# Order of small pieces of work around a fixed stream of matmuls: weight chunks, partial sums, table loads and loads of k

## The reference

```
ek = exp(min(k, 30));  ekv = ek * k;  euk = exp(min(u + k, 30))
nf, nb = forward and backward scans a = a * decay + ekv;  df, db = the same of ek
num = nf + nb - ekv + euk * k;  den = df + db - ek + euk
y = sigmoid(r) * num / max(den, 1e-8) * (0.8 + 0.2 * tf)
```

```
out = x + y @ W.T + bias + sum over experts of coeff[e] * (y @ A[e].T) @ B[e].T
```

## Time and profile before

| | us |
|---|---|
| median of 3 runs | 652.41 |
| profiled execution | 651.88 |
| its span | 650.0 |
| TensorE busy (matmul) | 586.4 |
| VectorE | 498.6 |
| ScalarE | 381.6 |
| GpSimd | 382.1 |

### The profile page before, as it was taken

One profiled execution on the slowest core, in us unless ns is written; L12 is line 12 of the kernel. 1 busy time (PEld: TensorE's weight loads), 2 busy tenths in 40 slices (PEclk: granted clock), 3 DMA queues, 4 the chain that ended last, 5 costly groups with the idle time before them and its releaser, 6 DMA issues.

```text
span 650.0 us, 6967 instructions
## 1 busy us (share of the span) xinstructions
PE 586.4 (90%) x2562; PEld 471.7 (73%) x2562; DVE 498.6 (77%) x546; ACT 381.6 (59%) x463; POOL 382.1 (59%) x201
## 2 busy tenths in 40 slices
PE   0155899999989999999899989999999999999997
PEld 0044686768867867888688867888788878888786
DVE  7999999999999999997989789997899131032202
ACT  6878899879768786759575966386355310020100
POOL 1999889899959955866665748575457200000100
PEclk9976999999999999999999999999999999999999
DMA  5534555548826721674042625565354503050112
GB/s 194 151 113 174 161 180 169 175 104 190 154 72 127 158 84 39 189 178 119 32 146 75 201 65 151 139 185 174 81 146 127 149 0 98 0 162 1 50 48 81
DMA packets 31090, 78.72 MB, mean 121 GB/s; under 512 B 4496, under 2 KB 4688, under 8 KB 31056
## 3 DMA queue, kind: packets, MB, share of 16 engines
q1 hardware_dynamic: 26304, 65.43, 31.3%
q0 software_dynamic: 4752, 12.85, 12.0%
HBM read 57.03 MB, written 29.62 MB: 133 GB/s over the span
## 4 chain that ended last, share of the span: by engine, by line
PE 40%; DVE 32%; POOL 9%; ACT 8%; issue 7%; DMA 3%; SPq 0%; POOLq 0%; ACTq 0%; DVEq 0%
PE acc L1146 13%; PE acc L1147 12%; PE acc L1148 12%; DVE mix L941 5%; DVE mix L932 5%; DVE mix L936 5%; DVE mix L963 4%; POOL mix L777 3%; DVE yr L970 3%; DVE kv L946 3%; POOL yr L758 2%; DVE eu L951 2%; POOL mix L752 2%; DVE mix L919 2%; ACT L589 1%
## 5 line engine op out<-in xcount | busy, mean ns | idle before, releaser
L1146 PE MATMUL acc<-y_hi,wa_hi 128*128 128x512 f32 x638 | 255.2, 400 | 47.9 <-POOL y_lo L787 41.4
L1147 PE MATMUL acc<-y_lo,wa_hi 128*128 128x512 f32 x638 | 251.7, 395 | 0.0
L1148 PE MATMUL acc<-y_hi,wa_lo 128*128 128x512 f32 x638 | 251.3, 394 | 0.0
L1146 PEld LDWEIGHTS acc<-y_hi,wa_hi 128*128 128x128 f32 x638 | 121.7, 191 | 78.6 <-POOL y_lo L787 43.4
L1148 PEld LDWEIGHTS acc<-y_hi,wa_lo 128*128 128x128 f32 x638 | 121.7, 191 | 26.1
L1147 PEld LDWEIGHTS acc<-y_lo,wa_hi 128*128 128x128 f32 x638 | 122.0, 191 | 24.5
L777 POOL TENSOR_TENSOR mix<-mix,kv 128x1024 f32<-128x1024 f32 x30 | 75.0, 2501 | 53.9 <-DVE mix L919 53.9
L787 POOL TENSOR_TENSOR y_lo<-yr,y_hi 128x1024 fp32r<-128x1024 f32 x31 | 76.1, 2454 | 35.1 <-ACT y_hi L464 35.1
L800 POOL TENSOR_TENSOR wx_lo<-xa,wx_hi 128x512 fp32r<-128x512 f32 x16 | 20.6, 1325 | 107.9 <-ACT wx_hi L552 107.9
L752 POOL TENSOR_TENSOR mix<-mix,kv 128x1024 f32<-128x1024 f32 x31 | 77.3, 2493 | 4.5 <-DVE mix L963 4.5
L984 DVE SCALAR_TENSOR_TENSOR xo<-acc,bias_sb,xo 128x512 f32<-128x512 f32 x32 | 23.7, 742 | 72.3 <-PE acc L1148 72.1
(11 more groups left out here) (138 smaller groups left out, 744.9 us busy)
## 6 DMA issues: line engine op xcount, KB each, us to landing
kv<-f_cm SPq DMA_DIRECT2D x32, 512.0 KB, 3.4
yr<-x_cm SPq DMA_DIRECT2D x32, 512.0 KB, 3.4
out<-xo SPq DMA_DIRECT2D x64, 256.0 KB, 4.1
out<-x_cm POOLq DMA_DIRECT2D x16, 512.0 KB, 7.6
xo<-x_cm SPq DMA_DIRECT2D x32, 256.0 KB, 3.9
out<-xo POOLq DMA_DIRECT2D x17, 256.0 KB, 6.7
xo<-w_base SPq DMA_DIRECT2D x4, 512.0 KB, 3.5
xa<-w_base SPq DMA_DIRECT2D x4, 512.0 KB, 4.3
```

Source lines behind the costliest of these rows:

```text
L1146: nc.tensor.matmul(out_ap, wh, yh, start=start, stop=False)
L1147: nc.tensor.matmul(out_ap, wh, yl, start=False, stop=False)
L1148: return nc.tensor.matmul(out_ap, wl, yh, start=False, stop=stop)
```

## The change

1. *Weights on GpSimd.* Chunk 6 goes ahead of `split_lo` in step 4 instead of behind it. Chunk 11 (step 8) is done in halves, the first ahead of `split_lo`. Second-place halves (chunk 3 in step 1, chunk 4 in step 2, chunk 11 in step 8) are cut into two operations of 256 columns.
2. *Partial sums.* Part 3 is copied in step 3 instead of 4, part 4 ahead of the inverse of step 4, part 7 at the end of step 4 instead of behind `exp_uk` of step 5, parts 10 and 11 one chunk sooner in step 6. Stores follow.
3. *SyncE* in steps 18 and 21: `load_k` ahead of the first store.
4. *ScalarE:* step 19 no longer counts as held, so `sigmoid_r(19)` stands in its usual place, ahead of `scale_end_den`; in step 23 `sigmoid_r` and `exps` stand behind `inverse`. In step 9 the turned weights are copied ahead of the table load. In step 25 (G = 4) `exp_gap` stands ahead of `copy_xa` and `copy_turned` right behind it.
5. *VectorE:* `weigh(4)` behind `forward(25)` instead of `forward_num(25)`.
6. *TensorE:* in G = 4 two units of tile 2 (six matmuls) go ahead of `turn`.

```diff
--- before.py
+++ after.py
@@ -121,10 +121,10 @@
         load_late_steps = [[], [], [], [7], [8], [], [], [12]]
         hi_steps = [[2, 3], [4], [5], [6], [7], [8], [9, 10], [11], [12]]
         hi_mid_steps = [[1]]
-        lo_steps = [[0, 1], [2], [], [5], [], [7], [8], [9], [], [12]]
-        lo_late_steps = [[], [], [], [], [6], [], [], [10], [11]]
-        lo_halves_steps = [[], [], [(3, 1), (4, 0)]]
-        lo_halves_late_steps = [[], [(3, 0)], [(4, 1)]]
+        lo_steps = [[0, 1], [2], [], [5], [6], [7], [8], [9], [], [12]]
+        lo_late_steps = [[], [], [], [], [], [], [], [10]]
+        lo_halves_steps = [[], [], [(3, 1), (4, 0)], [], [], [], [], [], [(11, 0)]]
+        lo_halves_late_steps = [[], [(3, 0)], [(4, 1)], [], [], [], [], [], [(11, 1)]]
 
         def chunks_at(table, s):
             return table[s] if s < len(table) else []
@@ -161,9 +161,9 @@
         ACT_OUT = 2 * PARTS
         PBUF = 4
         part_depth = [HALF - 1] * 5 + [HALF] * 3 + [HALF + 1] * 2 + [HALF + 2] * 6
-        PART_EXP_K, PART_CHUNK, PART_END, PART_EXP_UK = range(4)
-        parts_at = {(3, PART_CHUNK): (0, 3), (4, PART_CHUNK): (3, 5), (4, PART_END): (5, 7), (5, PART_EXP_UK): (7, 8), (5, PART_END): (8, 10),
-                    (6, PART_END): (10, 13), (7, PART_EXP_K): (13, 16)}
+        PART_EXP_K, PART_CHUNK, PART_END = range(3)
+        parts_at = {(3, PART_CHUNK): (0, 4), (4, PART_EXP_K): (4, 5), (4, PART_END): (5, 8), (5, PART_END): (8, 10),
+                    (6, PART_CHUNK): (10, 12), (6, PART_END): (12, 13), (7, PART_EXP_K): (13, 16)}
 
         LATE_DEPTH, LATE_SLOT, LATE = CB - 2, 2, SPLIT * CB + 3
         LATE_NEXT = next(e for e in range(PARTS, 2 * PARTS) if e % XBUF == LATE_SLOT)
@@ -215,8 +215,8 @@
         routing_at = {(first_step(G) + 1, AFTER_FWD): G for G in (5, 6, 7)}
         routing_at |= {(CB, AFTER_BWD_NUM): 0, (first_step(1) + 1, AFTER_FWD_NUM): 1, (first_step(3) + 1, AFTER_BWD_DEN): 3}
         routing_at |= {(THIRD, AFTER_FWD_NUM): SPLIT, (FIFTH + 1, AFTER_RATIO): 4}
-        weigh_at = {(first_step(G) + 1, AFTER_FWD_NUM): G for G in (4, 5, 6, 7)}
-        weigh_at |= {(CB + 1, AFTER_FWD): 0, (first_step(1) + 1, AFTER_BWD_DEN): 1, (THIRD, AFTER_BWD_DEN): SPLIT, (first_step(3) + 1, AFTER_SCALE): 3}
+        weigh_at = {(first_step(G) + 1, AFTER_FWD_NUM): G for G in (5, 6, 7)}
+        weigh_at |= {(FIFTH + 1, AFTER_FWD): 4, (CB + 1, AFTER_FWD): 0, (first_step(1) + 1, AFTER_BWD_DEN): 1, (THIRD, AFTER_BWD_DEN): SPLIT, (first_step(3) + 1, AFTER_SCALE): 3}
 
         def summed(G):
             return G + 1 - sum(1 for g in SUMMED if g < G)
@@ -396,21 +396,20 @@
             for s in range(STEPS):
                 G, q = quarter(s)
                 ended = ends_at.get(s, -1)
-                if 1 <= s < UNITS - 1 and ended in (SPLIT, SPLIT + 1):
+                k_first = ended in (SPLIT, SPLIT + 1) or (q == 2 and G in (SPLIT, SPLIT + 1))
+                if 1 <= s < UNITS - 1 and k_first:
                     load_k(s + 1)
                 if ended >= 0:
                     for j in range(3, 6):
                         store(ended * CB + j)
                 if q == 2 and G >= SPLIT:
                     store(G * CB)
-                if 1 <= s < UNITS - 1 and ended not in (SPLIT, SPLIT + 1):
+                if 1 <= s < UNITS - 1 and not k_first:
                     load_k(s + 1)
                 if s == THIRD - 1:
                     sp.wait_ge(late_part_out, 1)
                     sp.dma_start(at(out, LATE), xo[:, LATE_SLOT, :]).then_inc(late_part_stored, 16)
                 for p in tiles(parts_at, s - 1, PART_END):
-                    store_part(p)
-                for p in tiles(parts_at, s, PART_EXP_UK):
                     store_part(p)
                 for n in chunks_at(load_steps, s):
                     load_chunk(n)
@@ -603,7 +602,7 @@
 
             for s in range(STEPS):
                 G, q = quarter(s)
-                late_split, late_sigmoid = held(s - 1), held(s - 2)
+                late_split, late_sigmoid = held(s - 1), held(s - 2) and s != THIRD + 3
                 if s == THIRD:
                     split_late_hi(s - 1)
                     sigmoid_r(s)
@@ -625,8 +624,8 @@
                     copy_xa(0)
                     exp_gap(0)
                     sigmoid_r(s)
+                    copy_turned(0)
                     exps()
-                    copy_turned(0)
                     exp_uk(s)
                     scale_end_den(s)
                     split_wx(0)
@@ -645,12 +644,12 @@
                 if s < UNITS:
                     exp_uk(s)
                 drains(s, AFTER_EXP_UK)
-                for p in tiles(parts_at, s, PART_EXP_UK):
-                    drain_part(p)
+                if routed and G == 4:
+                    exp_gap(G)
                 if routed:
                     copy_xa(G)
                 if routed and G == 4:
-                    exp_gap(G)
+                    copy_turned(G)
                 if 0 < s < CB:
                     scale_end_den(s)
                 if s < UNITS and not routed and not late_sigmoid:
@@ -667,7 +666,7 @@
                 if 0 < s <= UNITS and not late_split:
                     split_hi(s - 1)
                 drains(s, AFTER_HI)
-                if routed and G != 3:
+                if routed and G not in (3, 4):
                     copy_turned(G)
                 if s < UNITS and not routed and not late_sigmoid:
                     exps()
@@ -688,7 +687,7 @@
                     drain_part(p)
                 if routed and G != 3:
                     split_wx(G)
-                if s < UNITS and late_sigmoid:
+                if s < UNITS and late_sigmoid and s != FIFTH - 1:
                     sigmoid_r(s)
                     exps()
                 if q == 0 and G == 0:
@@ -700,6 +699,9 @@
                     if s == 0:
                         act.wait_ge(gains_ready, 2)
                     inverse(s)
+                if s == FIFTH - 1:
+                    sigmoid_r(s)
+                    exps()
                 drains(s, AFTER_INVERSE)
                 if routed and G == 3:
                     split_wx(G)
@@ -734,11 +736,14 @@
                     nc.gpsimd.tensor_tensor(wb_lo[:, kind[1], :], s, wb_hi[:, kind[1], :].bitcast(fp32),
                                             ALU.subtract).then_inc(w_lo_ready, 1)
 
-            def half_lo(n, h):
-                k, c = chunks[n][1], slice(h * (D // 2), (h + 1) * (D // 2))
+            def half_lo(n, h, pieces):
+                kind, width = chunks[n], D // 2 // pieces
+                hi, lo = (wb_hi[:, kind[1], :], wb_lo[:, kind[1], :]) if kind[0] == "expert" else (
+                    wa_hi[:, kind[1], ER:ER + D], wa_lo[:, kind[1], ER:ER + D])
                 pool.wait_ge(w_hi_ready, n + 1)
-                last = nc.gpsimd.tensor_tensor(wa_lo[:, k, ER:ER + D][:, c], stage[n % 2][:, c],
-                                               wa_hi[:, k, ER:ER + D][:, c].bitcast(fp32), ALU.subtract)
+                for i in range(pieces):
+                    c = slice(h * (D // 2) + i * width, h * (D // 2) + (i + 1) * width)
+                    last = nc.gpsimd.tensor_tensor(lo[:, c], stage[n % 2][:, c], hi[:, c].bitcast(fp32), ALU.subtract)
                 if h:
                     last.then_inc(w_lo_ready, 1)
 
@@ -872,7 +877,7 @@
                 if s == THIRD + 3:
                     add_late()
                 for n, h in chunks_at(lo_halves_steps, s):
-                    half_lo(n, h)
+                    half_lo(n, h, 1)
                 for n in chunks_at(lo_steps, s):
                     weights_lo(n)
                 if 0 < s <= UNITS and not late_split and s - 1 not in HALVED:
@@ -884,7 +889,7 @@
                 for j in range(*x_rows_at.get(s, (0, 0))):
                     add_x_row(j)
                 for n, h in chunks_at(lo_halves_late_steps, s):
-                    half_lo(n, h)
+                    half_lo(n, h, 2)
                 for n in chunks_at(lo_late_steps, s):
                     weights_lo(n)
                 if q == 1 and G not in (SPLIT, 3):
@@ -1385,7 +1390,7 @@
                     for kc in range(4 if G == 4 else base_from(G, 1), CB):
                         base(G, 1, kc)
                 k2 = base_from(G, 2)
-                ahead = {0: CB - 1, SPLIT: CB - 1}.get(G, k2)
+                ahead = {0: CB - 1, SPLIT: CB - 1, 4: 2}.get(G, k2)
                 if ahead > k2:
                     pe.wait_ge(xa_copied, 2 * G + 1)
                     for kc in range(k2, ahead):
```

## The result

The changed kernel takes 647.67 us, the median of 4 runs (646.71 to 648.36), beside 652.38 for the kernel before: a ratio of 0.9919 [0.9903, 0.9936]. The prediction was 647.4 (645.0 to 650.3). The profiled execution took 648.36 with a span of 646.5, 3.5 less than before's 650.0; it is the slowest of the four.

A forecast was written before the change was run, and what follows sets the result against it. After 58 us TensorE's queue bounds the kernel, so only removed holes pay. Terms 1.9 + 0.7 + 1.8 + 0.4 + 0.2 = 5.0 us take the profiled 651.88 to 646.9; 0.53 for the median gives 647.4 (645.0 to 650.3).

The forecast's parts named there:

- Steps 1 to 3: Early steps: GpSimd, without idle time from 32.4 to 45.5 us, limits VectorE's lead to 0.85, then 0.5 us.
- V: VectorE's lead in us against the old trace, carried along the steps beside TensorE's lead.
- The rival that more comes early: Steps 1 to 3: GpSimd isn't the limit and VectorE keeps 1.2 us, giving 645.9; chance 0.10.
- T = 1.75 and V = 2.0 at step 6: Leads of TensorE (T) and VectorE after removed waits, including TensorE's 1.99 us hole at 75.19.
- The term for part 7's store: Step 5: no 2.30 us store wait before the end-scaling, so exp(k) comes earlier and VectorE gains 1.28 and 0.15.
- T = V = 2.6: Near 129 us: scale_e(9) and silu come earlier, the 0.69 hole goes, and TensorE and VectorE both lead by 2.6 us.
- The 0.7 that the new order of step 9 was to cost: At 142.5 us: x·A split 0.7 later, TensorE may stand 0.7 us more, regained at later waits.
- Step 19: Moved sigmoid_r(19): numerator's backward scan 2.05 us earlier despite waiting for r(19); TensorE's 1.81 hole at 313.04 goes.
- Slower: Rival: r(19) lands late, 8.9 us after issue using up the 5.0 gained; 653 at 9.5 us; chance 0.06.
- k(22) worth nothing: Steps 21 to 23: exp(k) comes 2.08 us earlier, but drains waiting for TensorE remove the gain by the end.
- Step 23: Inverse before sigmoid and loads: 1.35 us off the 2.89 wait before ratio(23); TensorE's 0.39 hole goes.
- Group 4: Routing at 380 to 398 us: 3.1 us of holes become one of some 3 before the experts, gaining 0.2.

The follow-up runs named there:

- no_pieces: Changed kernel with the late halves of chunks 3, 4 and 11 each in one operation of 512 columns again: 647.57 us.
- no_parts: Changed kernel with the old places for copying the partial sums and for their stores: 648.96 us.
- only19: Kernel before with only sigmoid_r(19) moved to its usual place: 650.00 us.
- no19: Changed kernel with step 19 held again, sigmoid_r(19) and its table loads behind exp_k(20): 650.92 us.
- no_k21: Changed kernel with SyncE's old order of load_k and store in steps 18 and 21: 647.43 us.
- no23: Changed kernel with sigmoid_r(23) and exps ahead of inverse(23) again: 648.80 us.
- no_g4: Changed kernel with all edits of group 4 undone (weigh, ScalarE's order, the six products): 646.32 us.
- weigh_back: Changed kernel with one edit undone, weigh(4) behind forward_num(25) again: 644.72 us.
- evac_sooner: Changed kernel with ScalarE's and GpSimd's splits of x·A for group 4 moved ahead, and tiles 32, 33 and 34 emptied sooner: 643.82 us.
- split_first: Changed kernel with ScalarE's split of x·A for group 4 ahead of its scan work, weigh left early: 644.91 us.

## Why the prediction was right, and where it was off

*Steps 1 to 3: right.* GpSimd is the limit. With `scale_e(2)` back at 0.79 us, `forward(3)` waits 0.23 for `p1(3)`, and V, 1.31 at 46, is 1.01 at 49 and 0.69 at 59 (predicted 0.85, then 0.5). The rival that more comes early is out. The 0.43 that part 3's copy was to cost ScalarE is there: VectorE waits 0.46 before `scale_e(5)`, and V is 0.14 at 72 (predicted −0.07). no_pieces has 0.00 there, so the gain of the pieces is nearly all given back by then.

*T = 1.75 and V = 2.0 at step 6: right, a little low.* No wait is left before part 8; before part 15 one of 0.30 is left where none was predicted; V is 2.44 at 87. The term for part 7's store (1.28 + 0.15) is right for before's trace, but it seems credited to the wrong edit: in no_parts that store lands in 2.2 us and the wait is gone with the old places of the copies. What the new places give is the hole before part 8, which costs about the same by another way, through ScalarE's copies of parts 8 and 9. They are worth 0.6 to 1.3.

*Steps 7 to 9, "T = V = 2.6": wrong.* V was 2.40 at 124 and 3.11 at 129, so `scale_e` and `silu` gave their 0.7. Then VectorE waits 0.80 at 130.98 for ScalarE's exponential of the gap (L537). ScalarE works without a gap from the split at 119.78 to 130.97, with the inverse, a chunk and the copies of x·A ahead of it, and earlier `silu` does not make this list shorter. V is 2.39 at 136, and the 0.7 are given back within 6 us. I had looked for what holds `silu` and not for what holds the next thing that VectorE takes from ScalarE. It hides in the sum because the lead before it was larger by as much. The 0.7 that the new order of step 9 was to cost before the experts at 142.5 is not there (0.27 for 0.23). The wait that grew by 0.7, from 1.33 to 2.03 at 137, is the one where TensorE, ahead by 0.7 more, meets VectorE, which is not.

*Step 19: right.* Gap 2.48 for 2.6, gain 2.10 for 2.05 at 298; r(19) landed 3.3 us after its issue, for 3.4. The sum had it at 1.8 at the hole of 313; only19 measures 2.25 and no19 3.25. The us more in no19 is, in its profiled execution, the clock behind the hole at 310.71 (some 1.55). The hole of 1.81 at the same place cost the kernel before no clock in its profile. So taking a hole away can also save what it costs in clock, which the sum did not have. In the rival *Slower* one figure is off: by the sum's own terms a landing of 8.9 us would leave VectorE under 1 us later at 298 than before, not 3.4.

*k(22) worth nothing: right, and shown.* V rises to 6.86 at 333, and falls because ScalarE's drains wait 3.52 us for TensorE and VectorE then 1.26 for ScalarE; no_k21 costs nothing.

*Step 23: right, the time less clear than the trace.* The wait before `ratio(23)` is 1.54 for 2.89, as predicted (1.35 off), and the 0.39 at 374 is gone. no23's trace gives it 0.5 by 392, where the sum had 0.4; the medians say 1.1.

*Group 4: right in the trace, the price incomplete.* Neither cat nor the turned copy is waited for, and one hole of 2.96 on wx_lo stands for 3.11: the +0.2 of the sum. What I did not see is that such a hole can cost the clock, 1.44 us here. The logits were already 4.90 us ahead at 376.14, so the group's edits add 0.2 before the hole's own costs and less than nothing behind them (no_g4). The place of `weigh` is what spoils them: with it undone the hole is 1.21 for 2.96, and weigh_back is 1.75 us faster for that and somewhat more for the clock. The prediction followed the chain that the move makes, and got its length right, but did not ask what the same edits would give without it.

That 647.4 stands so near 647.67 is partly luck. The sum against the profiled execution gave 646.9, and the profiled execution after took 648.36, 1.5 more, the size of the clock's loss. The sum has no term for the clock, and the median of 647.67 is the middle of four times, two near 647 and two near 648.3.

Open: what makes a hole cost the clock in one execution and not in the next; whether part 7's wait goes with the edit of the weights; whether the early `weigh` is needed for the 643.8 of evac_sooner, since weigh_back does as well as split_first; whether moving the exponential of the gap ahead of the copies in step 8 would save the 0.7 (not tried).

## What to carry to other kernels

TensorE keeps only as much lead as the engine that feeds it has, so follow two leads through the trace and, behind each wait that goes, look for the next thing that the feeding engine takes from a third. A move in one queue can cost if the consumers in the other queues stay: `weigh` moved alone put a hole of 1.62 us into the kernel before, and the changed kernel gains 2.8 us when ScalarE's split moves along (or `weigh` moves back, 3.0), and 3.9 when GpSimd's split and three emptyings of banks move too. Several short holes turned into one long one of equal sum need not be a draw: the long one can cost clock, and what is lost behind the last hole is lost for good, since nothing waits there. Before a difference between two kernels is explained by their waits, look at the granted clock behind each hole of both.

## What the runs showed of the hardware

- The granted clock fell to 1.2 GHz for some 3.4 us behind a hole of 2.96 us in one execution and not in another with the same hole; the same at 2.03 us (8 of 11) and at 1.86 to 1.99 (4 of 6), never in these traces at 1.81 or less. It cost 1.44 us where no wait followed, some 1.55 in no19 where the wait that followed hung on TensorE itself, and 0.25 at 137 us, where VectorE set the pace.
- VectorE's `scale_e` takes 0.74 us alone, 1.54 and 1.36 where GpSimd works on a piece of 512 columns, and 0.79 and 0.82 where that is cut in two: it gets in between two GpSimd operations that follow each other at once.
- The same 256 KB store landed in 4.7, 4.7 and 5.1 us in three executions in which a 512 KB load had been issued 1.3 us before it, and in 2.2 in one in which that load was issued 3.6 us before it. This decided whether a wait of 2.3 us existed.
